# A sequence block with attention and FFN branches: third layernorm's statistics ahead of the FFN gate, norm matmuls two chunks behind

## What is computed

```python
xn = _layernorm(x)                         # over the last axis, 1024
# attention branch
q, k, v = split(xn @ Wqkv + bqkv)          # 3 x 1024 columns
q = q / norm(q); k = k / norm(k)           # over the 1024 columns of each token
kv = sum(k * v, axis=tokens)               # one vector of 1024 for each batch row
attn = (q * kv) @ Wout + bout
# FFN branch, ternary weights with one scale for each output column
h = silu(xn @ w1.T * s1) * (xn @ w2.T * s2)      # 1024 -> 4096
h = gelu(h @ h1.T * sh1); h = gelu(h @ h2.T * sh2)  # 4096 -> 4096, twice
out = x + attn + h @ w3.T * s3                   # 4096 -> 1024
```

## Time and profile before

| | us |
|---|---|
| time, median of 2 runs | 3114.78 (3109.88 and 3119.68) |
| time of the profiled execution | 3107.64 |
| span of its slowest core, core 0 | 3105.8 |
| spans of the eight cores | 3070.8 to 3105.8 |
| PE busy on core 0 | 2889.8 (93%) |
| ACT, DVE, POOL busy | 464.8, 378.7, 219.9 |

### The profile page before, as it was taken

How to read it: one execution, slowest core, us unless ns; L and a number is a source line. 1 busy time by engine, 2 the same in 40 slices (tenths; PEclk the granted TensorE clock), 3 DMA queues, 4 the chain that set the end, 5 groups by cost and what they waited for, 6 DMA issues and landing times.

```text
span 3105.8 us, 30690 instructions; the slowest of 8 cores (3070.8 to 3105.8 us)
## 1 busy us (share of the span) xinstructions
PE 2889.8 (93%) x13056; PEld 1282.6 (41%) x13056; DVE 378.7 (12%) x440; ACT 464.8 (15%) x463; POOL 219.9 (7%) x420
## 2 busy tenths in 40 slices
PE   3889997669999999999998899999999999999997
PEld 0334442224444444444433344444444444444443
DVE  3254113333000000000002221100000000000011
ACT  1453112331000000000011031110000000000100
POOL 0000000000000000000000000000000000000000
PEclk8989998999999999999999899999999999999999
DMA  6554444655444444444455644444444444444453
GB/s 165 134 132 100 75 82 109 126 91 97 79 76 75 76 80 76 75 76 79 77 102 103 142 95 75 81 75 75 78 78 75 75 77 79 75 75 77 76 108 93
DMA packets 76598, 278.93 MB, mean 90 GB/s; under 512 B 8752, under 2 KB 8880, under 8 KB 76464
## 3 DMA queue, kind: packets, MB, share of 16 engines
q0 software_dynamic: 59904, 218.13, 41.9%
q1 hardware_dynamic: 16560, 58.85, 6.2%
HBM read 486.66 MB, written 8.39 MB: 159 GB/s over the span
## 4 chain that ended last, share of the span: by engine, by line
PE 82%; DMA 4%; ACT 2%; DVE 2%; issue 1%; SPq 0%; ACTq 0%; DVEq 0%
PE PD L198 23%; PE PC L198 23%; PE PA L198 18%; PE PB L198 18%; DMA xs<-x_fm 2%; DMA out_fm<-os 1%; ACT Gb L544 1%; ACT sq L555 1%; DVE os L689 1%; DVE os L683 0%; DVE tmp_f L577 0%; ACT os L655 0%; DVE tmp_f L573 0%; DVE xb L210 0%; ACT Ab L614 0%
## 5 line engine op out<-in xcount | busy, mean ns | idle before, releaser
L198 PE MATMUL PC<-Gb,wr 128*128 128x512 bf16 x2080 | 483.6, 385 | 27.0 <-DVE Gb L261 27.0
L198 PE MATMUL PD<-Gb,wr 128*128 128x512 bf16 x2080 | 478.0, 383 | 0.0
L198 PE MATMUL PB<-Gb,wr 128*128 128x512 bf16 x1728 | 392.3, 380 | 4.8 <-PEq L85 4.8
L198 PE MATMUL PD<-Ab,wr 128*128 128x512 bf16 x1536 | 359.1, 388 | 32.9 <-ACT os L655 32.9
L198 PE MATMUL PC<-Ab,wr 128*128 128x512 bf16 x1536 | 348.9, 380 | 2.0 <-ACT os L655 2.0
L198 PE MATMUL PA<-Gb,wr 128*128 128x512 bf16 x1536 | 347.2, 379 | 0.0
L198 PEld LDWEIGHTS PC<-Gb,wr 128*128 128x128 bf16 x2080 | 204.5, 99 | 280.4 <-issue 43.6
L198 PEld LDWEIGHTS PD<-Gb,wr 128*128 128x128 bf16 x2080 | 205.3, 99 | 248.8 <-issue 10.1
L198 PEld LDWEIGHTS PB<-Gb,wr 128*128 128x128 bf16 x1728 | 169.3, 98 | 210.3 <-issue 7.5
L191 POOL DMA_DIRECT2D wr<-h_t x256 | 135.1, 528 | 1622.4 <-PE PB L198 798.4
L198 PEld LDWEIGHTS PD<-Ab,wr 128*128 128x128 bf16 x1536 | 152.7, 100 | 224.6 <-issue 51.7
(11 more groups left out here) (82 smaller groups left out, 989.7 us busy)
## 6 DMA issues: line engine op xcount, KB each, us to landing
wr<-h_t POOLq DMA_DIRECT2D x256, 512.0 KB, 5.2
xs<-x_fm SPq DMA_DIRECT2D x96, 512.0 KB, 4.8
wr<-w_t POOLq DMA_DIRECT2D x96, 512.0 KB, 5.3
wr<-wqkv_t POOLq DMA_DIRECT2D x56, 512.0 KB, 5.9
out_fm<-os SPq DMA_DIRECT2D x16, 512.0 KB, 3.9
wr<-wout_t POOLq DMA_DIRECT2D x8, 512.0 KB, 6.3
cst<-consts SPq DMA_DIRECT2D x1, 64.0 KB, 1.8
ones_sb<-ones_bf SPq DMA_DIRECT2D x1, 32.0 KB, 2.6
```

The source lines that it names most:

```text
L198: e.matmul(p[:, h * 512:(h + 1) * 512], l, r, start=a, stop=b),
```

## The change

Two edits, both in block 2 and both for t = 0 alone.

1. `plan_stats(3, ...)` is called ahead of the gate stage instead of behind it, with `defer_xn=True`. The `xn` of group 3 (8 loads of x, 16 DVE instructions) stays where it was, behind the gate stage, since its region of `Gb` is read by the gate stage until then.
2. In the segments, the norm matmul of a chunk is put in a list `pend_sn` and issued two chunks later, behind the matmuls of chunk oc + 2. The last two of a segment are issued behind part "v".

```diff
@@ -454,6 +454,7 @@
                 t_rq = plan_q_rstd()
+                emit_xn3 = plan_stats(3, "PA", "PB", defer_xn=True) if t == 0 else None
                 qkvt_toks = plan_q_scale(t_rq) if t > 0 else None
@@ -506,7 +507,8 @@
                 if t == 0:
                     war[0] = S.pe_tok()
-                    plan_stats(3, "PA", "PB")
+                    for _c in range(DC):
+                        emit_xn3(_c)
@@ -518,6 +520,7 @@
                         norm_last2 = [None]
+                        pend_sn = []
@@ -551,16 +554,23 @@
                                     if part == "k":
+                                        if len(pend_sn) >= 2:
+                                            pend_sn.pop(0)()
                                         jq, qslot, fq = sq_ring.next()
                                         tq = S.op("scalar", lambda e, o=oc, qs=qslot, d=dst0: e.activation(
                                             qs[:, 0:512], Gb[:, d + o * 512: d + (o + 1) * 512], AF.Square),
                                             waits=[tkv, fq], inc="s_ac")
-                                        t_n = mm("PA", 0, ones_sb[:, :], qslot[:, 0:512],
-                                                 start=(oc == 0), stop=(oc == DC - 1),
-                                                 waits=[tq, psum_free["PA"]], inc="s_pe")
-                                        sq_ring.set_free(jq, t_n)
-                                        norm_last2[0] = t_n
+
+                                        def snmm(oc_=oc, jq_=jq, qslot_=qslot, tq_=tq):
+                                            t_n = mm("PA", 0, ones_sb[:, :], qslot_[:, 0:512],
+                                                     start=(oc_ == 0), stop=(oc_ == DC - 1),
+                                                     waits=[tq_, psum_free["PA"]], inc="s_pe")
+                                            sq_ring.set_free(jq_, t_n)
+                                            norm_last2[0] = t_n
+                                        pend_sn.append(snmm)
                                 w_ring.set_free(jw, last_tok)
+                        while pend_sn:
+                            pend_sn.pop(0)()
```

## The result

The changed kernel takes 3061.5 us (median of 11 runs) where the kernel before takes 3112.3 (10 runs in the same set): 51 us less where 69 were forecast, and just above the range of 3026 to 3060. In some executions the cores of one die show a lower granted clock (0.82 at the least) and the time is up to 16% longer, so every ratio, and every time from here on, is of the other runs alone, and an experiment with too few of those has no ratio. By them the ratio is 0.9836, 95% interval 0.981 to 0.9863, and the medians are 3057.0 and 3109.2 us, 52 us apart; 3057.0 lies just inside the range. So the total lies close to the upper bound, on one side or the other, and 1.6% is less than the 2% line of the prediction's chances.

The account below looks back on a forecast made before the run. TensorE was taken to bound the kernel. A gain of 102.9 us from the gate's end to h1 and a cost of 33.5 ahead of the gate gave -69.4, from 3112.4 to 3043 us; range 3026 to 3060.

Parts of the forecast that it names:

- 2% line: Whole kernel: smallest change a measurement can tell, at 3052.5 us; chances faster 0.71, same 0.27, slower 0.02.
- the norm matmuls: Tail of k and v: without the square's wait, matmuls take 117.4 us, plus 1.7 for h1's wait on Ln.
- 1.94 to 1.87 us race with DVE: Tail, part k: PE takes 1.94 us per chunk, DVE 1.87, so the deferred order goes on fitting.
- The start of segment 1: Tail: first square, 4.8 us after part v, is ready before its norm matmul, by under 1 us.
- the statistics behind the gate vanish: Gate's end to h1: 224.0 us becomes 121.1, gaining 102.9; ahead of the gate the statistics cost 33.5.
- about 30 us: Tail's start: expected time of the 16 DVE instructions for group 3's xn, which took 25.6 us before.
- the 2 us of lateness: Change from segment 0 to 1: k*v work late by 2 us; bounds 0 and 10, the latter with xn at 36.
- 2 us for the three weight loads ahead of the gate: Block 2's start: weight loads queued with the x loads add 2 us to the early statistics, within the 33.5.
- Early statistics as slow as at the kernel's start: Rival, ahead of the gate: 42 us instead of 33.5, x loads caught behind weight loads; 3052 us, chance 0.09.
- Weights as the bound: Rival, tail: weight units at 3.6 us make it 8 to 10 us longer; 3053 us, chance 0.13.
- the rival of a lower clock: Rival, tail: granted clock at 13/16 turns 117.4 us into 144.5; 3070 us, chance 0.02.
- the 5.95: Rival of slower or no gain, tail: weight loads barely overlap, deciding from about 5.95 us per unit; 3120 us, chance 0.03.

Follow-up runs that it names:

- two experiments: Changed kernel with group 3's xn chunks 6 and 7 behind segment 0's k*v work: 3047.5 us; changed kernel without segment 0's weight loads: 3040.0 us (one run).
- edit 2 alone: Against the kernel before, only the norm matmuls deferred, group 3's statistics left behind the gate: 3045.3 us, ratio 0.9793.
- last kernel: Changed kernel with group 3's statistics spread inside the gate and xn chunks 6 and 7 behind segment 0's k*v work: 3011.3 us, ratio 0.9688.

## Why the prediction was right or wrong

**Right: the norm matmuls.** Without the late xn, gate's end to h1 is 119.5 and 119.3 us in two experiments; the sum had 117.4 + 1.7. The two square slots, the order Ln behind the last evacuation (h1 waits 1.2 us for it, not 1.7) and the 1.94 to 1.87 us race with DVE held as argued: segments 2 and 3 show no wait. The start of segment 1, said to fit by under 1 us, misses by about 1 in those two experiments.

**Right: the statistics behind the gate vanish, and come back ahead of it uncovered.** The gate waits for L242, as named.

**Wrong: the term "about 30 us" for xn, and with it the 2 us of lateness.** It was 41.5 us, and the lateness 12 us, with nearly 2 us more for the matmuls at the lower clock behind it, which had no term at all: 132.8 instead of 121. This is the larger part of the miss, 12 of some 17 us by stage. The bound named for it, 36 us and 10 us, was too low as well.

The prediction had the facts. It found 117 us of DMA work in a tail of 117 us and asked only whether the weights would be late. The step that failed is averaging the DMA work over the whole tail: the x loads fall into its first 30 us. At the measured 3.2 us for a weight unit (0.706 x 35 us for 4.02 MB, 7.7 units) and 1.9 us for an x chunk (0.316 x 35 us for 5.8 chunks), the first segment asks for an estimated 8 x 3.2 + 8 x 1.9 = 41 us of DMA work in 29. (For an x chunk the prediction took half a weight unit, 1.6, which is a little low.) And it looked at the wrong victim. Weights have five slots, so a load is issued four units, some 15 us, before it is needed; x has two, and DVE waits for it in order. The weights took 13.2 us to land and PE did not wait for them; x took 10.3 and PE stood still.

**Wrong in size: 2 us for the three weight loads ahead of the gate.** They cost 6 to 8 (30.2 with them held back, 36.2 to 38.3 without). Without them the sum was a little high, 31.5 where 30.0 was measured. Their own DMA time, 3 x 3.2 = 9.7 us, was a better estimate than the difference to a stretch that had about one load beside it.

**The rivals.** Early statistics as slow as at the kernel's start had the right mechanism, x loads caught behind the weight loads, and 38 of its 42 us. Weights as the bound named the right resource and the wrong queue; no wait for `wr` over 0.4 us appeared in the tail. The granted clock was 1.00 in the dense stretch from 555 to 590, so the rival of a lower clock did not come true in the profiled execution. No experiment lets the weights run one after another, but their units were used every 3.67 us without a wait, which excludes the 5.95.

The Trainium skill ("DMA: Bandwidth & Descriptors", "Issuing engines are not separate DMA queues") says that DMAs of SP, ACT and POOL end up on the same 16 engines and interleave whichever engine issued them. The shares of q0 and q1, which add up to the whole, agree; I had used it for the total and not for the terms of the sum that went wrong.

The sign of edit 1 was not in the prediction at all: it took the two edits as one. The runs show that edit 2 alone is worth 64 us of stage length and edit 1 takes 14 of them back.

## What to carry to other kernels

Removing waits of TensorE raises the pace at which every stream is consumed, so budget the DMA engines for the stretch in which a load is needed, not for the stage, and ask which queue has the fewest slots: here the lateness landed there, not on the heaviest stream, and a third slot moved part of it back. Work moved off one wait into another place is only a gain if something covers it there; spread over a dense stage, 32 matmuls cost 8 us, and at a point where all engines had just met they cost 38. Where an in-order engine stands between two consumers, order its work by who waits first: two of eight chunks moved behind the urgent work were worth 13 us.

## What the runs showed of the hardware that was not expected

The DMA engines ran at a share of 0.97 over 123 us (last kernel, core 2) and TensorE did not wait for its weights there; with five slots, weight loads that landed after 13 us (changed kernel) in place of 5.9 were harmless. An x load's landing time went from 4.6 us without weight loads beside it (weights held back, core 7) to 10.2 beside a full weight queue and 12.0 with a third x load in flight (medians of the cores). A weight unit took 3.2 us of all 16 DMA engines, whether they were half busy (h1) or full.
